# Involution: the next image's norm and squeeze put between this image's products; attention tile with operands in PSUM

## The chip, the cores and the metric

The kernel runs on one core of one Trainium2 chip. The metric is the time of the whole kernel on the device, in microseconds (us).

## What is computed

Two blocks follow each other; each is a convolution-like part and then a mixture of experts whose gates come from graph attention over 524,288 edges and 32,768 nodes. The change touches the first block's convolution-like part (an involution) and the attention of both blocks. Cut to what matters:

```
# involution, images x of 8 x 128 channels x 64 x 64; xn = x normalised over channels
y = w1 @ xn + b1                                   # squeeze, 32 channels
y = depthwise3x3(y, wd) + bd
w = w2 @ y + b2                                    # 8 groups x 9 taps per pixel
out = x + sum over 9 taps (shifted xn * w[group, tap])

# graph attention, rows of `table` hold h (16 values), a_src (4), a_dst (4) of a node
e      = leaky_relu(a_src[src] + a_dst[dst], 0.2)  # per edge, 4 heads
alpha  = exp(e - segment_max(e, dst)) / segment_sum(exp(..), dst)
agg    = segment_sum(h[src] * alpha, dst)          # then layernorm, top 2, softmax -> gates
```

## The kernel before, in words

Everything on chip is float32 with 128 partitions. The stages follow each other with a full stop between them: the sort of layer 0's edges (about 0 to 961 us of the span), `involution` (961 to 2381), `heads` (the table of h, a_src, a_dst), `attention` of layer 0 (from 2692 to about 9000; its first part also holds `Ordering`, the sort of layer 1's edges), `experts`, the mamba stages, and then `heads`, `attention` and `experts` of layer 1.

**Involution.** An image is 8 tiles of 512 pixels. For each image the kernel first runs the norm and squeeze of all 8 tiles (function `tiles` with `nm.pe_mean`, `nm.pe_var`, `nm.act_square`, `nm.act_root`, `nm.dve_centre`, `nm.dve_scale`, lines 123 to 151): PE averages over channels (L127), DVE subtracts (L136), ACT squares (L140), PE averages the squares (L131), ACT takes logarithm and exponential (L145, L147), DVE scales into `xn` (L151), PE squeezes (L671), ACT adds the bias and writes three shifted copies into `y` (L701). Then come the products of all 8 tiles: PE makes the 72 kernel rows `kP` from `y` in three matmuls (L677), ACT adds a bias into `kern` (L707), PE spreads each of 9 taps to 128 partitions in one of three PSUM tiles `eP` (L684), DVE multiplies a tap with shifted `xn` (L739) and adds it into `acc` (L745). A tap's spread waits until the product three taps earlier is done. After a tile DVE also runs `bounds.turn` (L537, L539): POOL has fetched blocks of `dst` by indirect DMA (L526), DVE counts in them. SP loads one image at a time (L619) and stores `acc` by the tile (L626).

**Attention, first part.** POOL runs `Gather.fetch`: 4096 indirect DMAs per layer, each of which takes a column of 128 edge sources (an index column in SBUF, `ring`) and brings 128 rows of 24 values from `table` into `got` (L894). SP stores groups of 16 columns to `rows` in DRAM (L873). ACT loads tiles of C = 128 columns back into `gs` (L978); DVE and ACT work on a tile (32 per layer): compare neighbours in `dst` (`cont`, L997; `brk`, L999), carry a_dst along each partition by four scans (L1006), add a_src (L1010), leaky relu (L1012), running maximum by four scans (L1019), differences (L1022, L1023, L1025), two exponentials on ACT (L980, L981), h times weight (L1027), and 20 scans that sum (L1031). POOL's gathers wait for no result of DVE: they wait for their index columns and for a free half of `got` only.

A scan is `tensor_tensor_scan(out, data0, data1, initial, op0, op1)`; its `initial` is one value per partition, taken from the end of the last tile:

```
V.tensor_tensor_scan(out[:,par,1:C+1,f],dd[:,:,h],out[:,par,1:C+1,f],
    0.0 if begin else out[:,1-par,C,f:f+1],ALU.mult,ALU.add)        # L1031, 20 of them
```

Before the change all tiles of the attention's first part lie in SBUF (`r.sb`); only `Ordering` has PSUM there (4 banks of `turn`, `cntP`, `sideP`).

## Time and profile before

| | us |
|---|---|
| median of 3 runs | 20784.96 (20766.88 to 20813.07) |
| the profiled execution | 20795.29 |
| its span | 20793.7 |
| POOL busy, whole span | 10284.8 (49%) |
| DVE busy | 7812.9 (38%) |
| PE busy | 6756.5 (32%) |
| involution, from 961 to 2381: DVE, PE, ACT, POOL busy | 869.3, 1070.8, 299.8, 249.3 of 1420 |
| attention of layer 0, 4000 to 8000: POOL, DVE busy | 3106.1, 443.1 of 4000 |

No engine is busy for even half of the span, because the stages differ. What a change is worth is read stage by stage: who waits for whom there. Busy time of POOL counts the length of its gathers; the 0.30 us between two of them is not in it.

### The profile page before, as it was taken

The page shows a single profiled execution, that of the slowest core. Times are in us where ns is not written, and L with a number is a line of the kernel's source. Part 1 is how long each engine was busy: PE and PEld are TensorE (multiplying, and loading weights), DVE is VectorE, ACT ScalarE, POOL GpSimd, SP SyncE. Part 2 cuts the span into 40 slices and gives each one's busy share as a digit, 9 for nine tenths or more (in the row PEclk, how much of TensorE's full clock was granted, in tenths as well). Part 3 has the DMA queues.
Part 4 walks back from the last instruction along what each step waited for, and adds up shares of the span by engine and source line. Part 5 has one row for each costly group of instructions (what it writes and reads, how often), then busy time and mean ns, then how long its engine had stood idle before and what let it go on. Part 6 is the DMA issues. An engine that isn't in the chain of part 4 may idle for free. (4 is left out here: it accounts for less than half of the span.)

```text
span 20793.7 us, 223509 instructions
## 1 busy us (share of the span) xinstructions
PE 6756.5 (32%) x79070; PEld 3146.8 (15%) x79070; DVE 7812.9 (38%) x10937; ACT 3617.8 (17%) x6239; POOL 10284.8 (49%) x10259
## 2 busy tenths in 40 slices
PE   0277711000000000059789999740000000000079
PEld 0122301000000000024245555320000000000034
DVE  9866589111111111244478888510111111111244
ACT  0122201000000000023655555620000000000023
POOL 0011278777777777742100000147777777777710
PEclk8588855555555555579899999965555555555589
...
DMA packets 787024, 1072.74 MB, mean 52 GB/s; under 512 B 287476, under 2 KB 503636, under 8 KB 765652
## 3 DMA queue, kind: packets, MB, share of 16 engines
...
## 5 line engine op out<-in xcount | busy, mean ns | idle before, releaser
L894 POOL DMA_INDIRECT g_got<-table,g_ring x8192 | 8280.6, 1011 | 2496.9 <-issue 2496.9
L1118 PE MATMUL g_rowsP<-g_eye,g_meta 128*20 128x128 f32 x12 | 2.9, 416 | 10765.2 <-DVEq L1162 10765.2
L1010 DVE TENSOR_TENSOR g_z<-g_gs,g_pr 128x512 f32<-128x512 f32 x64 | 44.7, 699 | 8725.5 <-DMA g_gs<-rows 8725.5
L980 ACT ACTIVATE g_out<-g_u 128x512 f32<-128x512 f32 x64 | 40.3, 630 | 10747.0 <-DVE g_d L1025 10747.0
L1118 PEld LDWEIGHTS g_rowsP<-g_eye,g_meta 128*20 128x20 f32 x12 | 1.5, 142 | 10765.9 <-DVEq L1162 10765.4
L2070 POOL DMA_DIRECT2D m_x<-x x64 | 34.4, 537 | 2507.2 <-POOLq L1539 2500.8
L1359 PE MATMUL f_hP<-f_xn,f_w 128*128 128x512 f32 x2048 | 967.1, 595 | 699.4 <-DMA f_xn<-xn 699.4
L1366 PE MATMUL f_oP<-f_hid,f_w 128*128 128x512 f32 x2048 | 962.1, 592 | 0.0
L1388 ACT ACTIVATE f_hid<-f_hP,f_b 128x512 f32<-128x512 f32 x1024 | 647.5, 683 | 1122.3 <-PE f_hP L1359 1122.3
L526 POOL DMA_INDIRECT cb_got<-dst,k_blki x256 | 248.8, 972 | 1141.1 <-DVE cb_le L537 1078.1
L962 POOL DMA_INDIRECT ad<-g_nodes,k_start_row x512 | 695.6, 1359 | 182.3 <-issue 155.4
L1404 DVE SCALAR_TENSOR_TENSOR f_part<-f_oP,f_b,f_gate 128x512 f32<-128x512 f32 x512 | 384.5, 751 | 971.2 <-PE f_oP L1366 971.2
L684 PE MATMUL c_eP<-c_kern,c_pick 128*128 128x512 f32 x1152 | 585.0, 628 | 78.5 <-DVE c_prod L739 62.7
L1113 POOL DMA_INDIRECT g_tot<-state,k_last_row x512 | 507.7, 992 | 156.2 <-issue 156.2
L1031 DVE TENSOR_TENSOR_SCAN g_out<-g_dd,g_out 128x128 f32<-128x128 f32 x1280 | 575.1, 530 | 2.2
L1359 PEld LDWEIGHTS f_hP<-f_xn,f_w 128*128 128x128 f32 x2048 | 391.0, 191 | 1192.5 <-DMA f_b<-in_b 701.0
L526 POOL DMA_INDIRECT f0b_got<-dst,k_blki x256 | 241.5, 943 | 627.5 <-DVE f0b_le L537 564.6
L1695 PE MATMUL m_sg<-m_R,m_after 128*128 128x512 f32 x1024 | 513.5, 624 | 0.0
L517 POOL IOTA cb_pid_i<- 128x128 int32 x1 | 0.2, 234 | 961.5 <-POOLq L466 961.5
L296 DVE TENSOR_TENSOR s_keys<-s_keys 128x1024 f32<-128x1024 f32 (+1 forms) x354 | 462.8, 1307 | 13.2 <-ACT s_keys L447 6.4
L296 DVE TENSOR_TENSOR g0s_keys<-g0s_keys 128x1024 f32<-128x1024 f32 (+1 forms) x354 | 462.5, 1306 | 12.1 <-ACT g0s_keys L447 5.3
L1366 PEld LDWEIGHTS f_oP<-f_hid,f_w 128*128 128x128 f32 x2048 | 389.5, 190 | 489.6 <-issue 488.6
...
## 6 DMA issues: line engine op xcount, KB each, us to landing
g_got<-table,g_ring POOLq DMA_INDIRECT x8192
f_gate<-gates SPq DMA_DIRECT2D x128, 1024.0 KB
rows<-g_got SPq DMA_DIRECT2D x512, 192.0 KB, 1.9
...
h_x<-x SPq DMA_DIRECT2D x128, 256.0 KB
xn<-h_xn POOLq DMA_DIRECT2D x128, 256.0 KB
f_xn<-xn SPq DMA_DIRECT2D x128, 256.0 KB, 3.5
```

Of the source, the lines that this page charges most:

```text
L296: V.tensor_tensor(low_to,low(a),high(a),ALU.max if falls else ALU.min).then_inc(cmpd,1)
L526: pool.indirect_dma_start(self.got[:,par,k,:],None,self.dst_dram,bass.IndirectOffsetOnAxis(ap=self.keep.blki[:,c:c+1],axis=0)).then_inc(se ...
L684: nc.tensor.matmul(eP[k%3][:,:],picks[:,k,:],kern[:,par,:],start=True,stop=True).then_inc(spreadk,1)
L894: pool.indirect_dma_start(self.got[:,par,k,:],None,self.table,bass.IndirectOffsetOnAxis(ap=self.ring[:,par,k:k+1].bitcast(u32),axis=0)).th ...
L962: pool.indirect_dma_start(ad,bass.IndirectOffsetOnAxis(ap=keep.start_row[:,k:k+1],axis=0),nodes[:,k,20:24],None).then_inc(sent[par],16)
L1031: ins=V.tensor_tensor_scan(out[:,par,1:C+1,f],dd[:,:,h],out[:,par,1:C+1,f],0.0 if begin else out[:,1-par,C,f:f+1],ALU.mult,ALU.add)
L1113: pool.indirect_dma_start(tot[:,k,:],None,state_d,bass.IndirectOffsetOnAxis(ap=keep.last_row[:,k:k+1],axis=0)).then_inc(fetched[i],16)
L1359: last=nc.tensor.matmul(hP[e%2][:,f,:],w1s[:,e,f*P:f*P+P],xs[:,par,:],start=True,stop=True)
L1366: last=nc.tensor.matmul(oP[e%2][:,:],w2s[:,e,f,:],hid[:,e%2,f,:],start=(f==0),stop=(f==1))
L1388: last=nc.scalar.activation(hid[:,e%2,f,:],hP[e%2][:,f,:],ACT.Gelu,bias=b1s[:,e,f:f+1])
L1404: nc.vector.scalar_tensor_tensor(part[:,e%2,:],oP[e%2][:,:],b2s[:,e:e+1],gt[:,par,e,:],ALU.add,ALU.mult).then_inc(gated.sem,1)
L1695: TE.matmul(sg[c%2][:,:],after[:,:],R[:,c*16:c*16+16,:],start=True,stop=True).then_inc(segs.sem,1)
```

## The change

It has two parts.

In the involution, image 0's norm and squeeze run alone as before. After that, each of the 8 tile steps of an image also holds one tile of the next image's norm and squeeze. `image_used` and the function `tiles` go; slices are constants now, and a loop body holds two images. SP loads an image by tiles of 512 (8 DMAs instead of 1), each after the tile's place in the buffer has been read for the last time. The last image has no next one.

In the attention tile, the operands `cont`, `brk` (together `seam`), the carried a_dst and the running maximum (both `adm`), the leaky relu's small branch and the decay (both `low`), and the weight (`wP`) move to PSUM. DVE's leaky relu becomes a maximum of `z` and ACT's 0.2 z. ACT copies the maximum back to `out` and makes the weight twice. To free banks, `Ordering`'s `cntP` and `sideP` are laid into `turn`.

```diff
@@ Ordering
-self.cntP=r.pb("cntP",[P,HI])
-self.sideP=r.pb("sideP",[P,1])
+self.cntP=self.turn[:,1,0:2,:].rearrange("p a b -> p (a b)")
+self.sideP=self.turn[:,0,0,0:1]
...
@@ involution, PE
+def kernel_of(i,j,par,ip):
+    padded.of(pe,i+1 if j<TPI-1 else i)
+    biased.before(pe,i,1)
+    for kh in range(3):
+        last=nc.tensor.matmul(kP[:,:],wk[:,kh,:],y[ip][:,j*ROWS+kh:(j+1)*ROWS+kh,1:W+1],start=(kh==0),stop=(kh==2))
+    last.then_inc(kernels.sem,1)
+def image(b,ip,more):
+    on(kernel_of,b,0,ip)
+    if more: arrived(b+1,1-ip)
+    for j in range(TPI):
+        def spread(i,j,par,ip):
+            for k in range(row*3,row*3+3):
+                pe.wait_ge(times,i*9+k+1)
+                nc.tensor.matmul(eP[k%3][:,:],picks[:,k,:],kern[:,par,:],start=True,stop=True).then_inc(spreadk,1)
+        if more:
+            if j: on(squeeze,b+1,j-1,1-ip)
+            on(mean,b+1,j,1-ip)
+        biased.of(pe,b*TPI+j)
+        for row in range(3):
+            on(spread,b,j,ip)
+            if row==0 and j<TPI-1: on(kernel_of,b,j+1,ip)
+            if row==1 and more: on(var,b+1,j,1-ip)
+    if more: on(squeeze,b+1,TPI-1,1-ip)
...
@@ involution, ACT
+def image(b,ip,more):
+    on(add_bias,b,0,ip)
+    for j in range(TPI):
+        if more and j: on(pad,b+1,j-1,1-ip)
+        if j<TPI-1: on(add_bias,b,j+1,ip)
+        if more:
+            on(square,b+1,j,1-ip)
+            on(root,b+1,j,1-ip)
+    if more: on(pad,b+1,TPI-1,1-ip)
...
@@ involution, DVE (inside weigh, and its loop)
+            if k==2 and more:
+                on(centre,b+1,j,1-ip)
+                at.update(j=j,ip=ip)
...
+    for j in range(TPI):
+        on(weigh,b,j,ip)
+        if more: on(scale,b+1,j,1-ip)
...
@@ attention
-dd=r.sb("dd",[P,C,4])
+seam=r.pb("seam",[P,2,C])
+cont,brk=seam[:,0,:],seam[:,1,:]
+adm=r.pb("adm",[P,C,4])
+low=r.pb("low",[P,C,4])
+wP=r.pb("wP",[P,C,4])
...
+        shaped.of(act,i)
+        nc.scalar.activation(low[:,:,:],z[:,:,:],ACT.Copy,scale=0.2).then_inc(scaled.sem,1)
+        topped.of(act,i)
+        if not (isinstance(i,int) and i==0): nc.scalar.copy(out[:,par,0,20:24],out[:,1-par,C,20:24])
+        nc.scalar.copy(out[:,par,1:C+1,20:24],adm[:,:,:]).then_inc(kept.sem,1)
         shifted.of(act,i)
+        nc.scalar.activation(wP[:,:,:],u[:,:,:],ACT.Exp)
         nc.scalar.activation(out[:,par,1:C+1,16:20],u[:,:,:],ACT.Exp)
-        nc.scalar.activation(dd[:,:,:],d[:,:,:],ACT.Exp).then_inc(weighed.sem,1)
+        nc.scalar.activation(low[:,:,:],d[:,:,:],ACT.Exp).then_inc(weighed.sem,1)
...
-            ins=V.tensor_tensor_scan(pr[:,par,:,h],cont[:,:],ed[:,par,:,h],0.0 if begin else pr[:,1-par,C-1,h:h+1],ALU.mult,ALU.add)
+            ins=V.tensor_tensor_scan(adm[:,:,h],cont,ed[:,par,:,h],0.0 if begin else prc[:,1-par,h:h+1],ALU.mult,ALU.add)
+        V.tensor_copy(prc[:,par,:],adm[:,C-1,:])
         landed(dve,g_in,i,par)
-        V.tensor_tensor(z[:,:,:],gs[:,par,:,16:20],pr[:,par,:,:],ALU.add).then_inc(shaped.sem,1)
-        shaped.of(dve,i)
-        V.scalar_tensor_tensor(z[:,:,:],z[:,:,:],0.2,z[:,:,:],ALU.mult,ALU.max).then_inc(leaky.sem,1)
+        scaled.of(dve,i)
+        V.tensor_tensor(z[:,:,:],z[:,:,:],low[:,:,:],ALU.max).then_inc(leaky.sem,1)
...
-            ins=V.tensor_tensor_scan(out[:,par,1:C+1,20+h],brk[:,:],z[:,:,h],-FAR if begin else out[:,1-par,C,20+h:21+h],ALU.add,ALU.max)
+            ins=V.tensor_tensor_scan(adm[:,:,h],brk,z[:,:,h],-FAR if begin else out[:,1-par,C,20+h:21+h],ALU.add,ALU.max)
...
-        V.tensor_tensor(d[:,:,:],out[:,par,0:C,20:24],out[:,par,1:C+1,20:24],ALU.subtract).then_inc(fallen.sem,1)
-        V.tensor_tensor(u[:,:,:],z[:,:,:],out[:,par,1:C+1,20:24],ALU.subtract)
+        kept.of(dve,i)
+        V.tensor_tensor(u[:,:,:],z[:,:,:],adm[:,:,:],ALU.subtract)
+        V.tensor_tensor(d[:,:,:],out[:,par,0:C,20:24],adm[:,:,:],ALU.subtract).then_inc(fallen.sem,1)
         fallen.of(dve,i)
-        V.tensor_tensor(d[:,:,:],d[:,:,:],brk[:,:].unsqueeze(2).broadcast_to([P,C,4]),ALU.add).then_inc(shifted.sem,1)
+        V.tensor_tensor(d[:,:,:],d[:,:,:],brk.unsqueeze(2).broadcast_to([P,C,4]),ALU.add).then_inc(shifted.sem,1)
         weighed.of(dve,i)
-        V.tensor_tensor(out[:,par,1:C+1,0:16].rearrange("p c (h e) -> p c h e",e=4),gs[:,par,:,0:16].rearrange("p c (h e) -> p c h e",e=4),out[:,par,1:C+1,16:20].unsqueeze(3).broadcast_to([P,C,4,4]),ALU.mult).then_inc(spread.sem,1)
+        V.tensor_tensor(out[:,par,1:C+1,0:16].rearrange("p c (h e) -> p c h e",e=4),gs[:,par,:,0:16].rearrange("p c (h e) -> p c h e",e=4),wP[:,:,:].unsqueeze(3).broadcast_to([P,C,4,4]),ALU.mult).then_inc(spread.sem,1)
...
-            ins=V.tensor_tensor_scan(out[:,par,1:C+1,f],dd[:,:,h],out[:,par,1:C+1,f],0.0 if begin else out[:,1-par,C,f:f+1],ALU.mult,ALU.add)
+            ins=V.tensor_tensor_scan(out[:,par,1:C+1,f],low[:,:,h],out[:,par,1:C+1,f],0.0 if begin else out[:,1-par,C,f:f+1],ALU.mult,ALU.add)
```

PE in the product part of one image, before. `c_eP` is the spread of a tap, `c_kP` the kernel rows of the next tile; the piece shows the last spread of a tile, the next tile's kernel rows and the first spread behind them.

```order
L683 REGISTER_ALU
L684 MATMUL c_eP<-c_kern,c_pick 128x512
L37 ISA
L677 ISA
L677 MATMUL c_kP<-c_y,c_wk 72x512
L677 ISA
L677 MATMUL c_kP<-c_y,c_wk 72x512
L677 ISA
L677 MATMUL c_kP<-c_y,c_wk 72x512
L36 REGISTER_ALU
L683 ISA
L684 MATMUL c_eP<-c_kern,c_pick 128x512
```

PE in the same place with the change, between two tiles of an image that has a next one.

```order
L668 REGISTER_ALU
L669 MATMUL c_eP<-c_kern,c_pick 128x512
L655 MATMUL c_yP<-c_xn,c_w 96x512
L127 MATMUL c_n_mean<-c_img,c_mw 128x512
L668 ISA
L669 MATMUL c_eP<-c_kern,c_pick 128x512
L668 REGISTER_ALU
L669 MATMUL c_eP<-c_kern,c_pick 128x512
L668 REGISTER_ALU
L669 MATMUL c_eP<-c_kern,c_pick 128x512
L36 REGISTER_ALU
L660 MATMUL c_kP<-c_y,c_wk 72x512 x3
```

The next image's squeeze (`c_yP`) and mean (`c_n_mean`) now stand between the last tap of a tile and the first tap of the next. The squeeze waits for DVE's scale (L151), which stands behind the tile's last DVE instruction. The kernel rows moved from between two tiles to behind the third tap.

DVE in the loop of the attention tile, layer 0, before. `g_gs` are the gathered rows, `g_pr` the carried a_dst, `g_dd` the decay; all lie in SBUF.

```order
L1006 SCALAR_TENSOR_TENSOR g_pr<-g_cont,g_pr,g_ed 128x128 x4
L1010 TENSOR_TENSOR g_z<-g_gs,g_pr 128x512
L1012 SCALAR_TENSOR_TENSOR g_z<-g_z 128x512
L1017 COPY g_out<-g_out 128x4
L1019 SCALAR_TENSOR_TENSOR g_out<-g_brk,g_out,g_z 128x128 x4
L1022 TENSOR_TENSOR g_d<-g_out 128x512
L1023 TENSOR_TENSOR g_u<-g_z,g_out 128x512
L1025 TENSOR_TENSOR g_d<-g_d,g_brk 128x512
L1027 TENSOR_TENSOR g_out<-g_gs,g_out 128x128x16
```

The same place with the change. `g_seam`, `g_adm`, `g_low` and `g_wP` lie in PSUM, the others in SBUF.

```order
L1036 SCALAR_TENSOR_TENSOR g_adm<-g_seam,g_prc,g_ed 128x128 x4
L1039 COPY g_prc<-g_adm 128x4
L1041 TENSOR_TENSOR g_z<-g_gs,g_adm 128x512
L1043 TENSOR_TENSOR g_z<-g_z,g_low 128x512
L1049 SCALAR_TENSOR_TENSOR g_adm<-g_seam,g_out,g_z 128x128 x4
L1053 TENSOR_TENSOR g_u<-g_z,g_adm 128x512
L1054 TENSOR_TENSOR g_d<-g_out,g_adm 128x512
L1056 TENSOR_TENSOR g_d<-g_d,g_seam 128x512
L1058 TENSOR_TENSOR g_out<-g_gs,g_wP 128x128x16
L1062 SCALAR_TENSOR_TENSOR g_out<-g_low,g_out 128x128 x20
```

Each of these instructions, the first comparison (L1027, in front of the piece, with both inputs from `g_ds`) left aside, now has one tile at most from SBUF, besides a scan's initial value. The 4-element copy in front of the maximum scans is gone; one for the carried a_dst has come in.

## Rows read from the trace of the kernel before

**Rows 1.** The page's costliest groups: busy us, mean ns of one, idle before.

```profile
L894 POOL DMA_INDIRECT g_got<-table,g_ring x8192 | 8280.6, 1011 | 2496.9 <-issue 2496.9
```

**Rows 2.** Timeline of POOL, gathers of layer 1 (start, length, engine, line, what).

```profile
14160.76 0.97 POOL L894 DMA_INDIRECT g_got<-table,g_ring  x1 [0.30 <-issue]
...
19470.15 0.95 POOL L894 DMA_INDIRECT g_got<-table,g_ring  x1 [0.30 <-issue]
19490.11 0.94 POOL L894 DMA_INDIRECT g_got<-table,g_ring  x1 [0.30 <-issue]
```

**Rows 3.** Timeline of POOL beside one tile of layer 0.

```profile
5010.55 1.24 POOL L894 DMA_INDIRECT g_got<-table,g_ring  x1 [0.30 <-issue]
...
5017.18 2.55 POOL L894 DMA_INDIRECT g_got<-table,g_ring  x1 [0.30 <-issue]
5022.85 5.95 POOL L894 DMA_INDIRECT g_got<-table,g_ring  x1 [0.30 <-issue]
```

**Rows 4.** Timeline of DVE, the same stretch.

```profile
5010.29 0.69 DVE L1010 TENSOR_TENSOR g_z<-g_gs,g_pr 128x512 f32<-128x512 f32 x1 [140.83 <-DMA g_gs<-rows]
...
5016.63 2.29 DVE L1027 TENSOR_TENSOR g_out<-g_gs,g_out 128x2048 f32<-128x2048 f32 x1 [1.22 <-ACT g_dd L981]
5018.95 9.02 DVE L1031 TENSOR_TENSOR_SCAN g_out<-g_dd,g_out 128x128 f32<-128x128 f32 x20
```

**Rows 5.** Timeline of POOL, first and last gather of layer 0.

```profile
3230.21 1.93 POOL L894 DMA_INDIRECT g_got<-table,g_ring  x1 [0.30 <-issue]
...
8675.87 0.94 POOL L894 DMA_INDIRECT g_got<-table,g_ring  x1 [0.30 <-issue]
```

**Rows 6.** Busy time of the gathers in stretches of layer 0.

```profile
3230.20:3662.00 431.80, 353.67 (x257) 0.54 0.14 29
```

**Rows 7.** Timeline, POOL's fetches beside the involution's products on DVE.

```profile
1299.50 1.29 DVE L739 TENSOR_TENSOR c_prod<-c_eP,c_xn 128x512 f32<-128x512 f32 x2
1300.71 0.68 DVE L745 TENSOR_TENSOR c_acc<-c_img,c_prod 128x512 f32<-128x512 f32 x1
...
1299.77 0.94 POOL L526 DMA_INDIRECT cb_got<-dst,k_blki  x1 [8.16 <-DVE cb_le L537]
1301.02 1.19 POOL L526 DMA_INDIRECT cb_got<-dst,k_blki  x1 [0.30 <-issue]
```

**Rows 8.** POOL's fetches beside the expert stage; one of them beside L1404.

```profile
L526 POOL DMA_INDIRECT f0b_got<-dst,k_blki x256: 938/944/957, 9086.4 to 9954.2; - x128
...
9113.56 0.75 DVE L1404 SCALAR_TENSOR_TENSOR f_part<-f_oP,f_b,f_gate 128x512 f32<-128x512 f32 x1 [1.08 <-PE f_oP L1366]
...
9114.00 0.94 POOL L526 DMA_INDIRECT f0b_got<-dst,k_blki  x1 [0.30 <-issue]
```

**Rows 9.** Timeline of DVE: first centring and product, image 2's first, the stage's last reduce.

```profile
988.65 0.69 DVE L136 TENSOR_TENSOR c_n_cen<-c_img,c_n_mean 128x512 f32<-128x512 f32 x1 [2.61 <-PE c_n_mean L127]
...
1062.08 0.69 DVE L739 TENSOR_TENSOR c_prod<-c_eP,c_xn 128x512 f32<-128x512 f32 x1 [17.44 <-PE c_eP L684]
...
1163.08 0.69 DVE L136 TENSOR_TENSOR c_n_cen<-c_img,c_n_mean 128x512 f32<-128x512 f32 x1 [0.20 <-issue]
...
2375.23 0.42 DVE L539 TENSOR_REDUCE cb_within<-cb_le 128x256 f32 x1
```

**Rows 10.** Timeline of PE: one mean, then three kernel products at either clock.

```profile
986.39 2.07 PE L127 MATMUL c_n_mean<-c_img,c_mw 128*128 128x512 f32 x2 [13.76 <-DVE c_bias L727]
...
1396.76 5.40 PE L677 MATMUL c_kP<-c_y,c_wk 96*72 96x512 f32 x6 [2.16 <-ACT c_y L701]
...
1417.46 2.74 PE L677 MATMUL c_kP<-c_y,c_wk 96*72 x6
```

**Rows 11.** Stretches of the norm: PE idle, then a burst (clock after POOL's busy).

```profile
1516.00:1518.00 2.00, 0.00 (x0) 0.00 (x0) 0.69 (x1) 1.07 (x2) 0.00 (x0) 1.00 1.05 442
1519.00:1522.00 3.00, 3.00 (x5) 1.01 (x3) 0.35 (x1) 2.04 (x3) 0.00 (x0) 0.50 0.03 9
```

**Rows 12.** Timeline of ACT: the first exponential of a tile.

```profile
5015.44 0.63 ACT L980 ACTIVATE g_out<-g_u 128x512 f32<-128x512 f32 x1 [165.95 <-DVE g_d L1025]
```

More of the change, by code:

```diff
@@ L607, in involution, with images, on @@
         at={"j":0,"ip":0}
[L608 to L612 removed]
+        nm=Norm(nc,r,"n",mw[:,:],eps[:,0:1],lambda i,par: img[at["ip"]][:,at["j"]*T:(at["j"]+1)*T],lambda e,i,par: None,
+                lambda i,par: xn[at["ip"]][:,at["j"]*ROWS+1:(at["j"]+1)*ROWS+1,1:W+1],lambda e,i,par: None)
+        def images(eng, image):
+            with eng.Fori(0,B//2-1) as t:
+                for ip in range(2): image(t*2+ip,ip,True)
+            image(B-2,0,True)
+            image(B-1,1,False)
+        def on(f,b,j,ip):
+            at.update(j=j,ip=ip)
+            f(b*TPI+j,j,j%2,ip)
         @block.sync
@@ new lines, in arrived, with mean, var, squeeze @@
+            def arrived(b,ip): pe.wait_ge(img_in[ip],(b-ip)*64+128)
+            def mean(i,j,par,ip): nm.pe_mean(pe,i,par)
+            def var(i,j,par,ip): nm.pe_var(pe,i,par)
+            def squeeze(i,j,par,ip):
+                nm.normed.of(pe,i)
+                padded.before(pe,i,1)
+                nc.tensor.matmul(yP[:,:],w1s[:,:],xn[ip][:,j*ROWS+1:(j+1)*ROWS+1,1:W+1],start=True,stop=True).then_inc(squeezed.sem,1)
+            def kernel_of(i,j,par,ip):
[4 more added lines that the diff above has]
+                last.then_inc(kernels.sem,1)
@@ L686, in _ @@
+            arrived(0,0)
+            on(mean,0,0,0)
+            for j in range(TPI):
+                if j<TPI-1: on(mean,0,j+1,0)
+                on(var,0,j,0)
+                on(squeeze,0,j,0)
             images(pe,image)
@@ L727, in _, with centre, scale, arrived @@
             nc.vector.tensor_tensor(bias[:,:],kP[:,0:1],b2s[:,:],ALU.add).then_inc(w_ready,1)
-            def image(b,ip):
-                dve.wait_ge(img_in[ip],(b-ip)*8+16)
-                dve.wait_ge(edges,1)
-                tiles(dve,b,ip,lambda i,j,par,ip: nm.dve_centre(dve,i,par),lambda i,j,par,ip: nm.dve_scale(dve,i,par))
+            def centre(i,j,par,ip): nm.dve_centre(dve,i,par)
+            def scale(i,j,par,ip): nm.dve_scale(dve,i,par)
+            def arrived(b,ip): dve.wait_ge(img_in[ip],(b-ip)*64+128)
+            def image(b,ip,more):
+                if more: arrived(b+1,1-ip)
                 def weigh(i,j,par,ip):
@@ L753, in weigh @@
                     bounds.turn(dve,i,par)
-                tiles(dve,b,ip,None,weigh)
-                dve.sem_inc(image_used,1)
+                for j in range(TPI):
+                    on(weigh,b,j,ip)
+                    if more: on(scale,b+1,j,1-ip)
+            dve.wait_ge(edges,1)
+            arrived(0,0)
+            on(centre,0,0,0)
+            for j in range(TPI):
+                if j<TPI-1: on(centre,0,j+1,0)
+                on(scale,0,j,0)
             images(dve,image)
@@ L967, in _ @@
                 if order: order.scalar(act)
-                weighed.start(act)
+                for f in (scaled,kept,weighed): f.start(act)
                 for s in sent: act.wait_ge(s,HI//2*16)
```

127 lines of the change are left out of this document (42 added, 85 removed).

## The prediction

> **What bounds the kernel now.** First the page: of a span of 20,794 us the gathers of the two attention stages are 8280.6 us of POOL's busy time, and 2496.9 us of idle time before them have no other releaser than the issue [rows 1]. POOL waits for nobody there, so the pace of its gathers is the pace of both stages: about 5330 us each. I then read POOL's timeline where DVE is silent: 16 gathers from 19470.15 to 19490.11 are 1.2475 us apart, 0.945 long and 0.30 between [rows 2]. 4095 such steps are 5108.5 us. Layer 1 took 19490.11-14160.76=5329.4 [rows 2], which is 220.9 too much; layer 0 took 8675.87-3230.21=5445.7 [rows 5], 337.2 too much. What makes gathers long is seen by laying POOL's rows of one tile beside DVE's: the gather of 5017.18, issued inside the 2.29 us product L1027, took 2.55 and ended 0.81 behind that product; the one of 5022.85, issued inside the 20 scans L1031, took 5.95 and ended 0.83 behind the last scan [rows 3, 4]. A gather that meets DVE there is held until DVE is through. The three in the rows lose 0.30+1.61+5.01=6.92 us in a tile against a silent gather. 31 of a layer's 32 tiles lie beside gathers (the last needs the last gather); 62 times 6.92 is 429 of the 558 us lost in all.
>
> The involution is the second place: 988.65 to 2375.65 for 8 images, 173.4 us each. Image 1 takes 1062.08-988.65=73.4 for norm, squeeze and the first kernel rows, and 1163.08-1062.08=101.0 for its products, 12.6 a tile [rows 9]. The products keep DVE busy without a gap; in the norm all engines wait for each other.
>
> **Attention, step by step.** The change takes one of the two SBUF tiles away from each DVE instruction of the tile but L997. Whether that frees POOL is not shown in this stage; the nearest rows are two other places where POOL fetches beside DVE. In the involution a fetch issued at 1299.77 inside the products L739 (one input in PSUM, one in SBUF) took 0.94; the next, at 1301.02 inside the sum L745 (both in SBUF), took 1.19, 0.25 more [rows 7]. In the expert stage one issued inside L1404, with an input in PSUM, one in SBUF and a value per partition, the form that the scans will have, took 0.94, and none of 256 took over 0.957 [rows 8]. So I take the loss as gone. The Trainium skill's page "SBUF — State Buffer", section "Who interferes with whom", says the same for instructions with two SBUF inputs against a GpSimd instruction that reads SBUF; the same section also holds a rule against this change, which is a rival below.
> Layer 1: 220.9. Layer 0: the 257 gathers up to 3662 run beside the sort of the other layer's edges, which the change leaves alone [rows 6]; they lost 431.8-257x1.2475=111.2, and 337.2-111.2=226.0 remain. L997 stays with two inputs: 0.29 of each 1.25 us, a mean hold of 0.15, 64 times: about 2. **Gain 444.7.** Bounds: nothing (0) if PSUM does not matter; 446.9 if all goes.
> What is added costs time only where nobody gathers, in the last tile of each layer. Three ACT operations enter DVE's chain (0.2 z, the copy of the maximum, the second weight) at 0.63, 0.63 and some 0.6 (the length as in [rows 12]), the 4-element copy leaves: 1.9 us a layer, **4 in all**. Everywhere else a tile's DVE work, 18 us from its first row to the end of its scans [rows 4], and then some 25, is hidden under 160 us of gathers. Slower PSUM reads would be hidden too. Moving `cntP` and `sideP` adds no instruction and no wait: 0.
>
> **Involution, step by step.** What goes: 7 times the norm stretch. What comes: DVE has 2 more instructions a tile, PE 3 more matmuls, each two passes; ACT's 6 more are hidden (some 4.7 us of work in a tile, at about 0.65 each, the bias included [rows 12]). A pass takes 0.43 us at the full clock (2.4 GHz), 0.85 at half (1.2): 2.74 and 5.40 for six, less a tail [rows 10]. For PE's result to reach DVE I take 0.3, for DVE's to reach PE 0.2; the mean of 986.39, two passes of 0.85, released DVE at 988.65, 0.55 after its second pass, at the half clock [rows 9, 10].
> Count from DVE's scale of the next image's tile. It takes 0.7, the handover 0.2, and then PE has the squeeze, the mean and tap 0 in this order before DVE can multiply: six passes, 2.6, and 0.3 back. So DVE, until now never idle in a product tile, stands 3.1 us. From tap 0 to tap 3 PE has 12 passes (taps 1, 2, six passes of kernel rows, tap 3): 5.2, against 3.6 of DVE's work. From tap 3 on DVE is the slower: 12.6 less the five instructions done (3.0) is 9.5. Sum: 0.7+0.2+2.6+0.3+5.2+9.5=18.5 a tile.
> But PE is silent from tap 8 to the next squeeze, 5.2 us (behind tap 3 it has 12 passes, 5.2, against DVE's 9.5+0.9). In the norm stretch of before PE was silent from 1516 to 1518, still shown at 1.00; behind that it ran from 1519 to 1522 without a pause, at 0.50 [rows 11]. So the first five of my six passes run at half: 5x0.42=2.1 more, **20.6 a tile**. At an image's start six passes of kernel rows (2.6) and their bias with its handovers (1.2) lie open as well, less the mean beside them (0.9): 2.9. An image is 8x20.6+2.9=168. The stage: 73.4+7x168+101.0=1350.4 against 1387.0, **gain 36.6**. So little comes back because the interleaving trades 173.4-101.0=72.4 us of an image for 8 times 8.0 and 2.9. Bounds: PE at full clock all through gives 8x18.5+3=151, a gain of 156; half clock through the kernel rows too (12 more passes, 5.1 a tile) gives 208.5, a loss of 247.
> The 8 loads for 1 are issued on SP during an image and are complete before the next starts; the constant slices take out register instructions that cost nothing visible: both 0. If the last load came late, the start of an image would wait 2 to 3 us.
>
> **Sum.** 20795.3-444.7+4-36.6=20318.0 against the profiled execution. That lies 10.3 above the median, so **20308** for the median. About 0.2% (42 us) is what a measurement of this kernel can tell from no change.
>
> **The rivals.**
> *PE stays at the full clock.* For it: the kernel rows inside the products of before ran at it [rows 10]. Against: the long silence in each tile. 20308-7x17=20189.
> *The scans still hold POOL,* since their initial value and one input still come from SBUF and their output goes there. Against: L1404 has such a value too. 5.01 of each tile's 6.92 stay: 62x5.01=311, time 20619.
> *PSUM does not matter.* Then something else of DVE's activity holds POOL, and the stages keep their 445 us: 20753. For it: only a few rows of other places speak against. The same section of the Trainium skill infers that a `tensor_tensor` takes only the read side of what the two engines share while writing descriptors needs the write side, so that it should not stall a DMA of POOL's; the trace disagrees, L1027 held a gather for 1.61 [rows 3, 4]. By that rule alone the first part of the change would be worth nothing, which is this case's time.
> *Half clock through the kernel rows:* 20308+7x40.5=20592.
> *Slower.* One mechanism: PE at half clock for the whole of each interleaved tile. 0.9+5.1+0.3 to tap 0, 12 passes to tap 3 10.2, 12 more to tap 8 10.2, then DVE's last product, two sums, the count: 3.7. That is 30.4 a tile, 248 an image with what lies open at its start, 7x80=560 more: 20868, 0.4% slower even with attention's whole gain. It decides from about 29.9 us a tile. Against: 30 passes would be 26 us of nearly continuous work, and on such work the clock came back to full between 1396.76 and 1417.46 [rows 10].
>
> **How the numbers follow.** Forecast, with the involution from 20 us worse to 20 better: 0.73. Full clock 0.10, scans 0.09, PSUM without effect 0.04, half through the kernel rows 0.03, slower 0.01. The range reaches down to the full-clock case and up over the forecast by some 120, not half of the way to the next case: 20170 to 20430; it leaves out 0.17 and what little of the forecast lies beyond its ends. Every case but the last is faster: 20753 is only 32 us below the median, so part of its 0.04 counts as the same. Faster 0.97, same 0.02, slower 0.01.
>
> **What would show it.** Right: all gathers near 0.945 from 3662 on, each layer's gathers about 5112 (layer 1) and 5222 (layer 0) from first to last; DVE's tile longer by some us. In the involution an idle of 5 to 6 us before each tap 0, behind PE's squeeze and mean, PE's clock falling once a tile, and 165 to 171 us an image. Wrong: gathers of 3 to 6 us beside the scans; an image near 150 or above 173.

## The result, and the profile of the changed kernel

The changed kernel takes **20261.75 us** (median of 4 runs, 20240.76 to 20286.62) against 20786.44 of the kernel before (4 runs): a ratio of 0.9747, 95% interval 0.973 to 0.9764, so 2.5% faster. The forecast was 20308, with a range of 20170 to 20430. The profiled execution took 20261.57, its span 20260.0.

Gathers first. Here is the group of the profile's page that answers to [rows 1] (busy us, mean ns of one, idle before), and beside it the group of the involution's products, which now wait 395.3 us:

```profile
L916 POOL DMA_INDIRECT g_got<-table,g_ring x8192 | 7839.7, 957 | 2496.9 <-issue 2496.9
L751 DVE TENSOR_TENSOR c_prod<-c_eP,c_xn 128x512 f32<-128x512 f32 x576 | 393.5, 684 | 395.3 <-PE c_eP L669 394.5
```

8280.6 has become 7839.7, the mean 957 ns, and the 2496.9 us between gathers are the same. In the timeline of POOL the first and last gather of layer 0, then of layer 1:

```profile
3161.84 1.93 POOL L916 DMA_INDIRECT g_got<-table,g_ring  x1 [0.31 <-issue]
...
8384.70 0.94 POOL L916 DMA_INDIRECT g_got<-table,g_ring  x1 [0.30 <-issue]
...
13844.84 0.97 POOL L916 DMA_INDIRECT g_got<-table,g_ring  x1 [0.30 <-issue]
...
18956.08 0.94 POOL L916 DMA_INDIRECT g_got<-table,g_ring  x1 [0.30 <-issue]
```

That is 5222.9 us in layer 0 and 5111.2 in layer 1, against 5445.7 [rows 5] and 5329.4 [rows 2]: 440.9 us less. Behind layer 0's first 257 gathers, which run beside the sort, the longest of the other 7935 takes 0.97 us, where before 60 of them took over 3.9. Beside a tile of layer 0 (DVE, then POOL, to be laid beside [rows 3, 4]) no gather is longer than 0.95:

```profile
5040.51 0.69 DVE L1041 TENSOR_TENSOR g_z<-g_gs,g_adm 128x512 f32<-128x512 f32 x1 [131.69 <-DMA g_gs<-rows]
...
5048.73 2.29 DVE L1058 TENSOR_TENSOR g_out<-g_gs,g_wP 128x2048 f32<-128x2048 f32 x1 [1.70 <-ACT g_low L1011]
5051.05 8.77 DVE L1062 TENSOR_TENSOR_SCAN g_out<-g_low,g_out 128x128 f32<-128x128 f32 x20
```

```profile
5049.47 0.94 POOL L916 DMA_INDIRECT g_got<-table,g_ring  x1 [0.31 <-issue]
...
5051.96 0.95 POOL L916 DMA_INDIRECT g_got<-table,g_ring  x1 [0.30 <-issue]
```

DVE's chain from the first sum to the end of the scans is 19.3 us (5040.51 to 5059.82) instead of 17.7 (5010.29 to 5027.97 [rows 4]). It has grown, and the gathers' pace does not show it.

In the involution, one interleaved tile on DVE, from one scale of the next image to the next:

```profile
1288.75 0.68 DVE L151 TENSOR_TENSOR c_xn<-c_n_cen,c_n_rstd 128x512 f32<-128x512 f32 x1
1294.73 0.69 DVE L751 TENSOR_TENSOR c_prod<-c_eP,c_xn 128x512 f32<-128x512 f32 x1 [5.30 <-PE c_eP L669]
...
1299.89 0.69 DVE L751 TENSOR_TENSOR c_prod<-c_eP,c_xn 128x512 f32<-128x512 f32 x1 [1.21 <-PE c_eP L669]
...
1309.21 0.68 DVE L151 TENSOR_TENSOR c_xn<-c_n_cen,c_n_rstd 128x512 f32<-128x512 f32 x1
```

and on PE (squeeze, mean, taps 0 to 2, kernel rows, taps 3 to 5, variance, taps 6 to 8, the next squeeze):

```profile
1289.48 2.02 PE L655 MATMUL c_yP<-c_xn,c_w 128*96 128x512 f32 x2 [4.85 <-DVE c_xn L151]
1291.30 1.91 PE L127 MATMUL c_n_mean<-c_img,c_mw 128*128 128x512 f32 x2
1293.01 3.41 PE L669 MATMUL c_eP<-c_kern,c_pick 128*128 128x512 f32 x6
1296.25 2.74 PE L660 MATMUL c_kP<-c_y,c_wk 96*72 96x512 f32 x6
...
1302.27 2.74 PE L669 MATMUL c_eP<-c_kern,c_pick 128*128 128x512 f32 x6
1309.95 2.02 PE L655 MATMUL c_yP<-c_xn,c_w 128*96 128x512 f32 x2 [4.95 <-DVE c_xn L151]
```

Stretches around the next turn (us, PE busy, PEld, DVE, ACT, POOL, then PE's granted clock):

```profile
1305.00:1307.00 2.00, 0.00 (x1) 0.00 (x0) 2.00 (x4) 0.00 (x0) 0.00 (x0) 1.00 0.00 0
1307.00:1309.00 2.00, 0.00 (x0) 0.00 (x0) 1.42 (x4) 0.00 (x0) 0.00 (x0) 0.75 0.00 1
1309.00:1311.00 2.00, 1.05 (x2) 0.48 (x3) 0.90 (x2) 0.00 (x0) 1.15 (x1) 0.50 0.34 130
```

DVE waits 5.30 us before tap 0's product and 1.21 before tap 3's. PE is silent from 1305.0 to 1309.95, its clock is down when it starts again, and the squeeze and the mean take 2.02 and 1.91 us, where two passes at the full clock take 1.02 (as in experiment 6). A tile is 20.5 us here. The stage runs from 988.15 to 2301.19, 1313.0 us against 1387.0: 74.0 less. With the 440.9 that is 514.9 of the 533.7 us between the two spans; the rest lies in stages that the change hardly touches (24.8 less between the two layers' gathers, 6.1 more between the involution and the first gather). Neither is told from chance: over the thirteen traces of this case the first stretch takes 5443 to 5525 us and the second 851 to 861, whatever the version. The stage of the involution varies too, 1379.5 to 1387.5 us in three traces with the old one and 1311.2 to 1324.3 in seven with the new one, so that the gain of two executions laid side by side is 55 to 76, and 74.0 lies near the upper end.

### The profile page after: what moved, and what is told of

It is laid out like the page before. It is cut to its first block and busy times, and to the rows that moved or that the text cites. A ratio compares the mean times of both kernels' runs of the same rounds, so it can differ in the third digit from the quotient of the medians.

```text
span 20260.0 us, 221613 instructions
## 1 busy us (share of the span) xinstructions
PE 6675.2 (33%) x79070; PEld 3174.5 (16%) x79070; DVE 7799.2 (38%) x10939; ACT 3724.5 (18%) x6493; POOL 9847.2 (49%) x10259
## 5 line engine op out<-in xcount | busy, mean ns | idle before, releaser
L916 POOL DMA_INDIRECT g_got<-table,g_ring x8192 | 7839.7, 957 | 2496.9 <-issue 2496.9
L1041 DVE TENSOR_TENSOR g_z<-g_gs,g_adm 128x512 f32<-128x512 f32 x64 | 44.0, 687 | 8172.0 <-DMA g_gs<-rows 8172.0
L1062 DVE TENSOR_TENSOR_SCAN g_out<-g_low,g_out 128x128 f32<-128x128 f32 x1280 | 559.1, 529 | 2.3
L751 DVE TENSOR_TENSOR c_prod<-c_eP,c_xn 128x512 f32<-128x512 f32 x576 | 393.5, 684 | 395.3 <-PE c_eP L669 394.5
L296 DVE TENSOR_TENSOR g0s_keys<-g0s_keys 128x1024 f32<-128x1024 f32 (+1 forms) x354 | 461.2, 1303 | 12.2 <-ACT g0s_keys L447 5.4
```

The costliest lines, as they stand in the source:

```text
L296: V.tensor_tensor(low_to,low(a),high(a),ALU.max if falls else ALU.min).then_inc(cmpd,1)
L751: nc.vector.tensor_tensor(prod[:,k%3,:].rearrange("p (a b) -> p a b",b=W),eP[k%3][:,:].rearrange("p (a b) -> p a b",b=W),xn[ip][:,j*ROWS+k ...
L916: pool.indirect_dma_start(self.got[:,par,k,:],None,self.table,bass.IndirectOffsetOnAxis(ap=self.ring[:,par,k:k+1].bitcast(u32),axis=0)).th ...
L1062: ins=V.tensor_tensor_scan(out[:,par,1:C+1,f],low[:,:,h],out[:,par,1:C+1,f],0.0 if begin else out[:,1-par,C,f:f+1],ALU.mult,ALU.add)
```

## The experiments

The kernel before was timed again beside each group of experiments, with medians from 20772.22 to 20811.99; the changed kernel was timed once, when the kernel before had 20786.44. A difference from the changed kernel therefore carries some 15 us of this drift. In experiments 4 to 6 the difference of the two gains over the kernel before is given beside it.

**1. Each part alone.** One kernel has the diff's attention part (with the moved `cntP`, `sideP`) on the old involution, the other the involution part on the old attention tile.

```diff
 attention alone, e.g.
+adm=r.pb("adm",[P,C,4])
+low=r.pb("low",[P,C,4])
 involution alone, e.g.
+if j: on(squeeze,b+1,j-1,1-ip)
+on(mean,b+1,j,1-ip)
```

> The kernel before with the attention part of the change alone (and the moved cntP and sideP); the involution is the old one. My theory: the two parts do not touch each other, so this gains what the gathers lost beside DVE's instructions with two SBUF inputs: gathers first to last 5223 us in layer 0 and 5111 in layer 1, as with the whole change, some 441 us less than before in the two stages: about 20340 to 20350 for a median of before of 20786. Rival: part of the gather time's gain comes from elsewhere (the sort, the transfers), or the involution's change gives more than the 74 us that its stage shows; then this run is above 20380.

> The kernel before with the involution part of the change alone. My theory: the stage from first centring to last reduce takes 1313 us instead of 1387, as with the whole change, and nothing else changes: 20705 to 20720 for a median of before of 20786 (74 us less). An image takes 164 us, a tile 20.4. Rival: the two parts overlap in their effect (DMA traffic or clock left over from one stage to the next), so that this run gains under 40 or over 100 us.

Attention alone: 20350.04, ratio 0.9795 (0.9779 to 0.9812), 426.5 us less than 20776.57; gathers busy 7840.6 us as with the whole change. Involution alone: 20712.69, ratio 0.997 (0.996 to 0.998), 63.9 less. Together 490, against 525 for the whole change; the intervals (390 to 459, and 42 to 83) allow 432 to 542. In the traces the first kernel's gathers are 439.9 us shorter from first to last and the second's stage 67.7 us shorter. So nothing shows that the parts touch each other.

**2. The decay back in SBUF, and the decay alone in PSUM.** The first is the whole change without this one tile, the second the kernel before with this one tile.

```diff
 whole change, decay back
-nc.scalar.activation(low[:,:,:],d[:,:,:],ACT.Exp)
+nc.scalar.activation(dd[:,:,:],d[:,:,:],ACT.Exp)
-out[:,par,1:C+1,f],low[:,:,h],out[...]
+out[:,par,1:C+1,f],dd[:,:,h],out[...]
 kernel before, decay alone
-dd=r.sb("dd",[P,C,4])
+dd=r.pb("dd",[P,C,4])
```

> The whole change, but the decay (the second exponential of ACT, first input of the 20 scans) goes back to an SBUF tile; out, the other input, is in SBUF in either case. Theory A (a DVE instruction holds POOL's indirect DMA when both of its tensor inputs come from SBUF, whatever its form): the gather issued inside the 20 scans takes 5.5 to 6 us again, the others of the tile stay at 0.95; 31 tiles of each layer beside gathers, 5.0 us each, 311 us more: 20570. Theory B (what freed POOL is the PSUM output or the shorter products, not the scans' input): no long gather beside the scans, 20262 as with the whole change. The output's place is the same in both kernels, so a long gather here puts the cause on the input alone.

> The kernel before with one word changed: the decay tile (the second exponential's output, first input of the 20 scans) lies in PSUM. Nothing else of the change. My theory: the hold beside the scans goes (5.01 and twice some 0.15 in each of 62 tiles, 311 to 330 us), the 1.0 to 1.6 beside the product and the 0.1 to 0.45 beside the small ones stay: gathers 7950 to 7970 us busy instead of 8281, the kernel 20450 to 20470 against 20780. It would be three quarters of the attention part for one tile. Rival (the stretch of the product makes the gather late anyway and the hold moves to it or to the other scans): gain under 200.

Decay back in SBUF: 20605.26 (0.9916, 0.99 to 0.9933), 344 more than the changed kernel, gathers busy 8160.2, 320.5 more. In the timeline of DVE and of POOL, layer 1:

```profile
15074.13 2.29 DVE L1059 TENSOR_TENSOR g_out<-g_gs,g_wP 128x2048 f32<-128x2048 f32 x1 [1.74 <-ACT g_dd L1012]
15076.45 9.03 DVE L1063 TENSOR_TENSOR_SCAN g_out<-g_dd,g_out 128x128 f32<-128x128 f32 x20
```

```profile
15074.96 0.94 POOL L916 DMA_INDIRECT g_got<-table,g_ring  x1 [0.30 <-issue]
...
15077.45 1.25 POOL L916 DMA_INDIRECT g_got<-table,g_ring  x1 [0.30 <-issue]
15079.01 1.04 POOL L916 DMA_INDIRECT g_got<-table,g_ring  x1 [0.30 <-issue]
15080.35 5.94 POOL L916 DMA_INDIRECT g_got<-table,g_ring  x1 [0.30 <-issue]
```

The gather of 15080.35, inside the scans, is held until they end, 5.0 us, while the product in front of them, with its weight in PSUM, holds none (15074.96). The decay alone in PSUM: 20484.1 (0.9845, 0.9828 to 0.9861, against 20811.99 of the kernel before beside it, 328 less), gathers 7984.0, 296.6 less than before, and the gather at the product keeps its 1.6. I had forecast 20450 to 20470 and 7950 to 7970. So one word in one line is worth two thirds of the attention part by the gathers (296.6 of 440.9; three quarters by the whole times, 328 of 426.5), and the other tiles the rest.

**3. What holds a gather.** DVE has over 120 idle us in each tile beside gathers, so blocks of further instructions can be put there in layer 1. The first such kernel:

```diff
+for k in range(4): V.tensor_tensor(pP[:,k,:],pa[:,:],pc[:,:],ALU.add)
+for k in range(6): V.tensor_copy(po[:,k,:],pa[:,:])
+for k in range(6): V.tensor_scalar(po[:,6+k,:],pa[:,:],2.0,1.0,ALU.mult,ALU.add)
+for k in range(6): V.tensor_tensor(po[:,12+k,:],pa[:,:],pc[:,:],ALU.add)
```

> The whole change, and in each of layer 1's 32 tiles, while DVE would stand idle beside the gathers, 22 more DVE instructions of 128x512: 4 sums of two SBUF tiles into PSUM, 6 copies SBUF to SBUF, 6 tensor_scalar (times 2, plus 1) SBUF to SBUF, 6 sums of two SBUF tiles into SBUF. They add nothing to the result. Theory A (two SBUF inputs hold POOL): gathers beside the 4 sums into PSUM are held some 2 us and beside the last 6 sums some 3 us (as long as DVE runs them back to back), those beside the copies and tensor_scalar stay at 0.945 us. Then layer 1's gathers take 32 times about 5 us longer, 160 us. Rival 1 (the output's place counts too): the 4 sums into PSUM hold nothing, only the last 6 do. Rival 2 (any fast SBUF to SBUF form takes the shared way, as the Trainium skill's page "SBUF — State Buffer", section "Who interferes with whom", would have it for copies in a faster mode and not for tensor_tensor): the copies and tensor_scalar hold POOL, the sums do not.

```profile
15019.14 2.50 DVE L1055 TENSOR_TENSOR g_pP<-g_pa,g_pc 128x512 f32<-128x512 f32 x4
15021.54 2.19 DVE L1056 COPY g_po<-g_pa 128x512 f32<-128x512 f32 x6
...
15025.77 3.77 DVE L1058 TENSOR_TENSOR g_po<-g_pa,g_pc 128x512 f32<-128x512 f32 x6
```

```profile
15019.85 1.39 POOL L916 DMA_INDIRECT g_got<-table,g_ring  x1 [0.30 <-issue]
...
15024.18 1.09 POOL L916 DMA_INDIRECT g_got<-table,g_ring  x1 [0.30 <-issue]
...
15026.97 0.94 POOL L916 DMA_INDIRECT g_got<-table,g_ring  x1 [0.30 <-issue]
```

Gathers 7866.0 us busy, 26.3 more where I expected 160. The sums into PSUM held one gather by 0.45, the six sums into SBUF none: my theory as I had worded it (two SBUF inputs hold a gather as long as DVE runs them back to back) is wrong. The copies and `tensor_scalar`, 0.36 us each where a sum takes 0.63, stretched three gathers to 1.09. The Trainium skill ("SBUF — State Buffer", "Who interferes with whom") names just these as instructions that can take the port pair shared with GpSimd; the trace agrees that they delay its gathers, by 0.15 us each. The second kernel has long rows and long instructions:

```diff
+for k in range(20): V.tensor_tensor(po[:,k,:],pa[:,0:512],pc[:,0:512],ALU.add)
+for k in range(4): V.tensor_tensor(four(k),pa[:,:],pc[:,:],ALU.add)
+for k in range(4): V.tensor_tensor(four(k),pP[:,:],pc[:,:],ALU.add)
+for k in range(5): V.tensor_copy(four(k),pa[:,:])
```

> The whole change, and in each of layer 1's 32 tiles four blocks of DVE instructions beside the gathers, with a completion wait between blocks: 20 sums of 128x512 of two SBUF tiles (12 us in a row), 4 sums of 128x2048 of two SBUF tiles, 4 sums of 128x2048 of a PSUM and an SBUF tile, 5 copies of 128x2048 in SBUF; all contiguous, outputs in SBUF. The probe before showed no gather held by 6 short sums in a row (3.8 us). Theory A (two SBUF inputs hold a gather, but between short instructions it slips in for the first 3 to 4 us, as beside the old scans, whose first three gathers were held only 0.2 and 0.1): one gather is held for about 8 us to the end of the 20 sums, and one about 2 us or more by the 4 long sums; none by the sums with a PSUM input. Theory C (what held POOL was the form: the scans, or their strided tiles of 96 bytes a step): all sums leave the gathers at 0.945. The copies: each gather beside them 0.15 longer, as in the probe before, or held for a whole instruction.

```profile
15025.39 12.47 DVE L1057 TENSOR_TENSOR g_po<-g_pa,g_pc 128x512 f32<-128x512 f32 x20
15037.90 8.90 DVE L1060 TENSOR_TENSOR g_po<-g_pa,g_pc 128x2048 f32<-128x2048 f32 x4
15046.83 8.88 DVE L1063 TENSOR_TENSOR g_po<-g_pP,g_pc 128x2048 f32<-128x2048 f32 x4
15055.74 5.77 DVE L1066 COPY g_po<-g_pa 128x2048 f32<-128x2048 f32 x5
```

```profile
15026.20 1.29 POOL L916 DMA_INDIRECT g_got<-table,g_ring  x1 [0.30 <-issue]
...
15039.03 1.97 POOL L916 DMA_INDIRECT g_got<-table,g_ring  x1 [0.30 <-issue]
...
15057.40 1.97 POOL L916 DMA_INDIRECT g_got<-table,g_ring  x1 [0.30 <-issue]
```

A sum of 2.2 us with two SBUF inputs holds a gather until it ends (the gather of 15039.03 ends at 15041.00, 0.9 us behind the start of the second sum), and so it gets through at the boundary to the next; the same sum with one input in PSUM holds none in 8.9 us. Twenty short sums hold only the first, by 0.35. Theory A's gather of 8 us did not come. What then lets the old 20 scans hold one for 5 us? Two more kernels with rows of 128x128 instructions, all in SBUF:

```diff
 third
+for k in range(20): V.tensor_tensor_scan(po[:,k,:],pa[:,:],pc[:,:],0.0,ALU.mult,ALU.add)
+for k in range(20): V.tensor_tensor(po[:,k,:],pa[:,:],pc[:,:],ALU.add)
+for k in range(20): V.tensor_tensor_scan(ps[:,:,k],p4[:,:,k%4],ps[:,:,k],0.0,ALU.mult,ALU.add)
+for k in range(20): V.tensor_tensor(ps[:,:,k],p4[:,:,k%4],ps[:,:,k],ALU.mult)
 fourth
+for k in range(20): V.tensor_tensor_scan(ps[:,:,k],p4[:,:,k%4],ps[:,:,k],p0[:,0:1],ALU.mult,ALU.add)
+for k in range(40): V.tensor_tensor(po[:,k,:],pa[:,:],pc[:,:],ALU.add)
+for k in range(20): V.tensor_tensor_scan(po[:,k,:],pa[:,:],pc[:,:],p0[:,0:1],ALU.mult,ALU.add)
+for k in range(40): V.tensor_tensor_scan(po[:,k,:],pa[:,:],pc[:,:],0.0,ALU.mult,ALU.add)
```

> The whole change, and in layer 1's 32 tiles four blocks of 20 DVE instructions of 128x128, all tiles in SBUF, beside the gathers, with a completion wait between blocks: scans of contiguous tiles (initial value a constant), sums of contiguous tiles, scans in place with the steps of the kernel's own (16 bytes for the first input, 96 for the second and the output), products in place with those steps. The second probe showed that a sum of two SBUF tiles holds a gather to the end of the sum that runs, and that the next instruction lets it through; the old 20 scans held their third gather to the end of all 20. Theory D (a scan does not let go between two scans): both scan blocks hold a gather to the end of the block, the sums and products do not. Theory E (the 96-byte steps do it): the last two blocks hold one to their end, the first two do not. Theory F (it hangs on the initial value per partition that the old scans read, which no block here has): no block holds a gather for longer than one instruction.

> As the third probe, with other blocks in layer 1's tiles, 128x128, all tiles in SBUF: 20 strided scans in place (16 and 96 bytes a step) whose initial value is read per partition from SBUF, as the kernel's old scans do; 40 sums of contiguous tiles (0.21 us apart); 20 contiguous scans with such an initial value; 40 contiguous scans with a constant one. In the third probe strided scans with a constant initial value held each gather 0.30 at most, contiguous scans hardly at all, and 20 contiguous sums held their second gather 1.98 to the block's end. Theory F (a value per partition read from SBUF closes the gap between two scans): the first and the third block hold a gather to the block's end, as the old scans did, the fourth holds none. Theory G (it is a matter of beat, how far apart the instructions start, whatever their form): the first block, whose scans then start 0.45 apart as the old ones, holds one to its end; the 40 sums hold their second gather to their end, some 6 us; the third block only if its pitch changes too.

The fourth kernel, DVE's first two blocks and POOL's two longest gathers:

```profile
15102.28 9.02 DVE L1060 TENSOR_TENSOR_SCAN g_ps<-g_p,g_ps 128x128 f32<-128x128 f32 x20
15111.33 8.16 DVE L1063 TENSOR_TENSOR g_po<-g_pa,g_pc 128x128 f32<-128x128 f32 x40
```

```profile
15105.72 6.40 POOL L916 DMA_INDIRECT g_got<-table,g_ring  x1 [0.30 <-issue]
...
15113.75 6.56 POOL L916 DMA_INDIRECT g_got<-table,g_ring  x1 [0.30 <-issue]
```

Over the last three kernels, by the distance between the starts of two instructions in the row ("contiguous": the values of a tile lie side by side; "strided": 16 and 96 bytes apart). The third column says by how many us gathers were held, typically over 32 tiles:

| block | apart, us | gathers |
|---|---|---|
| 20 or 40 sums, contiguous | 0.21 | second held to the block's end: 2.0, 5.6 |
| scans, contiguous | 0.32 | 0.02, once 0.17 |
| scans, contiguous, initial value from SBUF | 0.38 | 0.2 to 0.26 each |
| strided scans, strided products | 0.39 | 0.30 each |
| strided scans, initial value from SBUF | 0.45 | third held to the end: 5.5 |
| sums 128x512 (second kernel) | 0.62 | first 0.35, then none |
| sums 128x2048 (second kernel) | 2.22 | to the end of one: 1.0 each |

Theories D (scans), E (96-byte steps) and F (initial value from SBUF) each fall by a row: contiguous scans hold hardly anything, strided scans 0.30, scans with an initial value 0.26 at most, and plain sums shut a gather out. The distance in time (theory G) goes with what is seen, but seven rows with no law between them are a description: why 0.21 and 0.45 shut a gather out and 0.32 to 0.39 do not stays open. It was not needed for the change: one input in PSUM let every gather through. The gathers of both layers are busy for 8065.8, 8001.0 and 8236.3 us in the second, third and fourth kernel, against 7839.7 in the changed one.

**4. Filling PE's silence.** Nothing reads what the five matmuls write.

```diff
+if more:
+    padded.before(pe,(b+1)*TPI+j,1)
+    for _ in range(5): nc.tensor.matmul(yP[:,:],w1s[:,:],picks[:,0:4,:],start=True,stop=True)
```

> The whole change, and five matmuls (128 to 96, 512 columns, two passes each) whose result nobody reads are issued on PE behind tap 8 of each interleaved tile, into the squeeze's PSUM tile before the squeeze writes it anew. They fill 4.3 of the 5.0 us in which PE is silent. My theory: the clock then stays at 1.00, the five slow passes of squeeze, mean and tap 0 cost 0.43 instead of 0.85 us, DVE waits 3.2 instead of 5.3 before each tap 0: 56 times 2.1=118 us less, 20145. Rival: the clock falls in spite of them, or the slow passes hide something else that is late then: 20262 as with the change.

20122.81 (0.9685, 0.9671 to 0.97), 139 less than the changed kernel; its gain over the kernel before is 649 where the change's is 525, 125 more. The stage takes 1176.8 us, 136 less. PE's clock across the former silence, and DVE's wait before tap 0:

```profile
1254.00:1261.00 7.00, 6.44 (x16) 2.33 (x15) 5.44 (x10) 0.00 (x0) 1.15 (x1) 1.00 0.10 37
```

```profile
1244.86 0.69 DVE L754 TENSOR_TENSOR c_prod<-c_eP,c_xn 128x512 f32<-128x512 f32 x1 [2.91 <-PE c_eP L669]
```

The clock stays at 1.00 and the wait is 2.91 instead of 5.30: 2.4 a tile (3.1 for an image's first), and all waits of the products for PE together fall from 394.5 to 260.0. Five matmuls more make the kernel faster. As nothing else of PE's work or order is changed, this is the price of the clock; the forecast had 2.1 a tile.

**5. Order on PE.**

```diff
-if more:
-    if j: on(squeeze,b+1,j-1,1-ip)
-    on(mean,b+1,j,1-ip)
 biased.of(pe,b*TPI+j)
 for row in range(3):
     on(spread,b,j,ip)
+    if row==0 and more:
+        if j: on(squeeze,b+1,j-1,1-ip)
+        on(mean,b+1,j,1-ip)
     if row==0 and j<TPI-1: on(kernel_of,b,j+1,ip)
```

> The whole change, with one thing moved on PE: the squeeze and the mean of the next image stand behind tap 2, in front of the kernel rows, instead of in front of tap 0. My theory: the wait before tap 0 (5.3 us in each of 56 tiles) goes, since taps 0 to 2 are spread while DVE does products 6 to 8; behind the scale PE has 10 passes and tap 3 before DVE can do product 3: 0.2+12 passes of 0.43+0.3=5.7 against 3.6 of DVE's work, so a wait of 2.1 to 2.5 before tap 3 instead of 1.2. A tile 15.7 to 16, 4.4 to 4.7 less; 56 times that, 250 less: 20000 to 20020. Rival (the wait is PE's amount of work, not its order): the time moves to the wait before tap 3, and less than 100 us are gained.

20078.78 (0.9665, 0.965 to 0.968), 183 less than the changed kernel (169 by the gains over the kernel before) where 250 were expected. PE, DVE and the clock (after POOL's column) between a scale at 1256.18 and the next tile:

```profile
1239.92 2.02 PE L655 MATMUL c_yP<-c_xn,c_w 128*96 128x512 f32 x2 [2.19 <-DVE c_xn L151]
1241.73 1.74 PE L127 MATMUL c_n_mean<-c_img,c_mw 128*128 128x512 f32 x2
```

```profile
1246.95 0.69 DVE L751 TENSOR_TENSOR c_prod<-c_eP,c_xn 128x512 f32<-128x512 f32 x1 [2.75 <-PE c_eP L669]
...
1256.18 0.68 DVE L151 TENSOR_TENSOR c_xn<-c_n_cen,c_n_rstd 128x512 f32<-128x512 f32 x1
```

```profile
1256.90:1260.30 3.40, 3.38 (x4) 1.32 (x5) 3.05 (x5) 1.31 (x2) 2.67 (x3) 0.51 0.20 41
```

The wait before tap 0 is gone inside an image. But after only 2.1 us of silence the squeeze and the mean again ran at 0.51, 3.4 us for 4 passes, so the wait before tap 3 is 2.75 and the centring waits 0.55 as well: a tile takes 17.0 us (1239.18 to 1256.18), not 15.7 to 16. I had counted these passes at the full clock.

**6. The work woven evenly.** `row(kh)` is one of the three matmuls of the next kernel rows; ACT's order follows PE's. The kernel rows of an image's first tile are now made in the last tile of the image before.

```diff
+for k in range(3): tap(k)
+if more: on(mean,b+1,j,1-ip)
+if j==0: on(squeeze,b,TPI-1,ip)
+elif more: on(squeeze,b+1,j-1,1-ip)
+tap(3)
+tap(4)
+row(0)
+tap(5)
+row(1)
+tap(6)
+row(2)
+tap(7)
+tap(8)
+if more: on(var,b+1,j,1-ip)
```

> The whole change with another order on PE and ACT, the same work in all. PE: taps 0, 1, 2, the next image's mean, the squeeze, tap 3, tap 4, first kernel row matmul, tap 5, second, tap 6, third, taps 7 and 8, the next image's variance. The kernel rows of an image's first tile are made in the last tile of the image before it, and its eighth squeeze in its own first tile. So PE can spread taps 0 to 2 while DVE still does products 6 to 8, and nothing stands between DVE's scale and its next product. My theory: with 30 passes of 0.43 at the full clock (12.9 us) against DVE's 20 instructions of 0.60 and 1.3 for the turn (13.3), DVE becomes the bound: a tile 13.3 to 13.6 instead of 20.4, an image 107 to 109 instead of 164, PE's clock never falls; 7 times 55 to 57 us less than with the change: 19865 to 19880. Rival: PE can't keep up with 13.4 us (its taps wait for products, the handovers add), a tile of 15 us or more, 19960 or above. Second rival: the attention stages or others are slower after it by some of this, for instance since the DMA traffic of the involution is closer together.

**19878.09** (5 runs, 19849.92 to 19890.52; 0.9564, 0.9551 to 0.9577): 384 less than the changed kernel (369 by the gains over the kernel before), as forecast (19865 to 19880), and the fastest version here. Two scales of the next image, then PE around one of them:

```profile
1207.54 0.68 DVE L151 TENSOR_TENSOR c_xn<-c_n_cen,c_n_rstd 128x512 f32<-128x512 f32 x1
1221.14 0.68 DVE L151 TENSOR_TENSOR c_xn<-c_n_cen,c_n_rstd 128x512 f32<-128x512 f32 x1
```

```profile
1247.50 1.02 PE L127 MATMUL c_n_mean<-c_img,c_mw 128*128 128x512 f32 x2
1249.36 1.10 PE L655 MATMUL c_yP<-c_xn,c_w 128*96 128x512 f32 x2 [0.84 <-DVE c_xn L151]
1250.30 1.88 PE L670 MATMUL c_eP<-c_kern,c_pick 128*128 128x512 f32 x4
```

and the waits of DVE's products for PE from 1044 to 1810 (us in total, times, longest):

```profile
DVE c_prod L763 <- PE c_eP L670: 3.5, 7, 1.2
```

DVE's products wait 3.5 us for PE in seven images, where in the changed kernel they wait 394.5 in eight. The first centring is at 988.34, the last reduce ends at 1906.93: 918.6 us, PE's mean clock 0.98. Gathers are unchanged (7839.5). What is left in these seven images is DVE's own work: from 1044 to 1810 it is busy for 730 of 766 us.

## Why the prediction was right

The forecast lay 46 us too high and well inside its range. Its larger part, attention, came out to 1%; of the smaller one the mechanism was right and the size half of what was measured.

**Attention.** Forecast 444.7, measured 440.9 in the trace, 426.5 (390 to 459) in the run of that part alone. Each layer's gathers came out at 5222.9 and 5111.2, forecast 5222 and 5112. The step that carried it, from fetches beside L739 and L1404 [rows 7, 8] to the tile, held for every form: sums, scans with an initial value in SBUF, the long product. The chain grew by 1.6, forecast 1.9; from layer 1's last gather to the end of the span stand 1303.9 us against 1303.6, but this stretch varies from 1301.8 to 1305.3 over the traces, so that the 4 us that the sum added for it cannot be told from nothing. The 2 us left for the comparison with two SBUF inputs (0.29 us long) did not show.

The reason given for the old loss was only half right. A gather is not held whenever DVE has two SBUF inputs: it is held to the end of the instruction that runs, and in some rows of short ones to the end of the row (experiment 3). The sum did not depend on it, since it took the old loss from POOL's own clock.

**The rivals there.** *PSUM does not matter*: fell, and with it, for these gathers, the inference told in the prediction from the Trainium skill ("SBUF — State Buffer", "Who interferes with whom") that a `tensor_tensor` does not stall a DMA of GpSimd: a sum of two SBUF tiles held gathers by 1.0. But each of these gathers reads an index column in SBUF; a DMA of GpSimd without one was not tried beside such a sum. *The scans still hold POOL*: fell; it was rightly priced, though: the decay back in SBUF costs 320.5 us of gathers and 344 of the whole time, forecast 311.

**Involution.** The mechanism was right, the size off: forecast gain 36.6, measured 74.0. The sum of the prediction was 73.4+7x168+101.0=1350.4.

- 73.4 for the first image's norm was taken over as it stood; it measured 61.2 (988.15 to 1049.32). Before, PE made the kernel rows of two tiles ahead of the first spread, 12 passes at half clock; now it makes one's, and from the last scale to the first product stand 8.1 us instead of 18.1. That was in the diff and I costed it at nothing: 12.2 of the 37.4. Part of this is chance: two other traces with the old involution have 68.3 and 69.3 instead of 73.4, with fewer of the 12 passes at half clock, while the new one's stays between 59.4 and 62.7. About 8 are the change's, and some 4 the clock's in that one execution.
- 7x168=1176 measured 1153.5 (1049.32 to 2202.86), 164.8 each: 22.5. Within a tile the steps held: wait before tap 0 5.3 (forecast 5.2 for handovers and passes), from tap 0 to tap 3 5.16 (5.2), from there to the scale 9.3 (9.5). Seen from the first product of each, the first seven tiles of an image came 20.35 apart, forecast 20.6; the eighth has no kernel rows behind its third tap and took some 19.0, which I had overlooked; the first waits 8.9, forecast 8.1.
- 101.0 for the last image measured 98.3: 2.7.

Between 1049 and 2203 PE, DVE and ACT never wait for a load of an image, so the loads by tile, which the sum put at nothing, cost nothing that the trace shows; they were not tried by themselves.

**The clock.** PE falls once a tile, as forecast, and filling the silence gave 139 us where the rival *PE stays at the full clock* had put 119 (125 by the gains over the kernel before). Half clock through the kernel rows and the slower rival did not come within an image: the kernel rows at 1296.25 took 2.74, the full clock. At the start of an image they did run at half, behind a silence of 5.5 us and the squeeze: the six passes that began at 1207.93 took 4.98 us, where the forecast had 2.6.

The 46 us are these: 37.4 from the involution, 18.8 from stages that the change hardly touches, where the two executions happen to differ, less the 10.3 by which the profiled execution of before was put above the median. Attention's two terms (444.7 gained where 440.9 came, and 4 added for the longer chain that did not show) cancel.
